# Hybrid block, software pipeline of 16 batches: the three filling steps rewritten with their own banks, places and orders, LayerNorms of those steps applied on ScalarE, and PSUM fetches of the draining steps moved to VectorE

## The reference

```python
x = x + attn_a(layernorm(x), w_qkv, w_out, b_out)   # 16 heads of 64: softmax(q*scale) over features,
                                                    # softmax(k) over tokens, context = q^T k per head,
                                                    # out = context applied to v, then @ w_out + b_out
x = x + ffn(layernorm(x), W_r, W_k, W_v, mu_r, mu_k)  # sigmoid(xr W_r) * (relu(xk W_k)^2 W_v)
                                                    # xr, xk: mu * x + (1 - mu) * (x shifted by a token)
x = x + attn_b(layernorm(x), W_Q, W_K, W_V, W_O)    # 16 heads of 8, rotary, softmax(q k^T / sqrt 8) v
x = x + ffn(layernorm(x), ... same weights)
```

## Time and profile before

| what | us |
|---|---|
| median of 3 runs (1088.19 to 1089.76) | 1088.46 |
| the profiled execution | 1087.98 |
| its span, first to last instruction of the program | 1086.2 |
| PE busy | 977.4 (90%) |
| ACT busy | 779.6 (72%) |
| DVE busy | 620.6 (57%) |
| POOL busy | 420.5 (39%) |

### The profile page before, as it was taken

The page is one execution under the profiler, slowest core; times in us unless marked ns, Lnnn a source line. Parts: engine busy times, 40 slices in busy tenths (PEclk is TensorE's granted clock), DMA queues, the critical chain, the costliest instruction groups (busy, mean ns, idle before and its releaser), DMA issues.

```text
span 1086.2 us, 21449 instructions
## 1 busy us (share of the span) xinstructions
PE 977.4 (90%) x8311; PEld 537.0 (49%) x8311; DVE 620.6 (57%) x1508; ACT 779.6 (72%) x905; POOL 420.5 (39%) x306
## 2 busy tenths in 40 slices
PE   3786798999999999999999999999999999999983
PEld 2565443545455454545455454545455454443322
DVE  4467644656675655656675655656675645564221
ACT  2343467787878687787878688787878687789861
POOL 3453534252625343352625344352625343223000
PEclk9899899999999999999999999999999999999985
DMA  5011121222223131222223131222222131322300
GB/s 152 20 31 49 50 80 38 70 68 72 75 59 98 54 97 37 72 68 69 78 60 97 55 97 36 73 65 72 75 60 88 51 90 37 96 66 84 83 24 15
DMA packets 61938, 72.25 MB, mean 67 GB/s; under 512 B 12289, under 2 KB 38786, under 8 KB 61826
## 3 DMA queue, kind: packets, MB, share of 16 engines
q1 hardware_dynamic: 61826, 70.75, 22.3%
HBM read 16.19 MB, written 20.97 MB: 34 GB/s over the span
## 4 chain that ended last, share of the span: by engine, by line
PE 66%; ACT 14%; DVE 12%; issue 4%; POOL 2%; SPq 1%; DMA 0%; ACTq 0%; DVEq 0%; POOLq 0%
PE PS L1279 17%; PE PS L1096 7%; PE PS L1235 6%; PE PS L1098 5%; PE PS L1097 5%; PE PS L1091 4%; ACT work L539 4%; PE PS L1152 4%; PE PS L1196 3%; PE PS L1203 3%; PE PS L1173 3%; ACT hn L567 2%; PE PS L1190 2%; ACT work L544 2%; ACT work L546 2%
## 5 line engine op out<-in xcount | busy, mean ns | idle before, releaser
L539 ACT ACTIVATE work<-PS 128x2048 f32<-128x2048 f32 x208 | 390.6, 1878 | 0.5 <-PE PS L1235 0.4
L533 ACT ACTIVATE work<-PS 128x512 f32<-128x512 f32 x256 | 152.6, 597 | 206.2 <-PE PS L1098 203.4
L1279 PE MATMUL PS<-work,v 128*32 128x512 f32 x2048 | 275.5, 610 | 2.8 <-DVE U L866 2.3
L375 POOL TENSOR_TENSOR rs<-ve,half_neg 128x4 f32<-128x4 f32 x64 | 65.3, 1020 | 368.1 <-DVE ve L724 368.1
L388 POOL TENSOR_TENSOR work<-work,q_rcp 128x1024 f32<-128x1024 f32 x64 | 121.8, 1903 | 173.0 <-DVE q_rcp L776 172.9
L1096 PE MATMUL PS<-wqk,h1h 128*128 128x512 f32 x256 | 123.0, 481 | 27.4 <-ACT gate L577 13.4
L1235 PE MATMUL PS<-q_st,k_st 32*128 32x512 f32 x832 | 105.6, 497 | 0.2
L1098 PE MATMUL PS<-wqk,h1l 128*128 128x512 f32 x256 | 102.8, 401 | 0.0
L1097 PE MATMUL PS<-wqk,h1h 128*128 128x512 f32 x256 | 102.4, 400 | 0.0
L773 DVE TENSOR_REDUCE q_sum<-work 128x16 f32<-128x1024 f32 x64 | 77.7, 1213 | 26.9 <-ACT work L533 26.7
L1152 PEld LDWEIGHTS PS<-work 128*64 128x64 f32 x2048 | 66.1, 140 | 47.3 <-ACT work L533 32.8
(11 more groups left out here) (144 smaller groups left out, 1667.7 us busy)
## 6 DMA issues: line engine op xcount, KB each, us to landing
qkv_scratch<-qkv_sb SPq DMA_DIRECT2D x16, 768.0 KB, 3.6
k_st<-k_hi SPq DMA_DIRECT2D x128, 64.0 KB, 2.1
k_st<-k_lo SPq DMA_DIRECT2D x128, 64.0 KB, 2.1
q_st<-q_hi SPq DMA_DIRECT2D x128, 64.0 KB, 2.1
q_st<-q_lo SPq DMA_DIRECT2D x128, 64.0 KB, 2.1
...
```

The source lines that it names most:

```text
L375: pool.tensor_tensor(rs[:, :], ve[:, :], half_neg[:, :], ALU.pow).then_inc(rstd[n].sem, 1)
L533: act.activation((EQ, EK)[r // 2][c % 2][:, (r % 2) * 512:(r % 2) * 512 + 512], PS[:, bank, :], ACT.Exp)\
L539: act.activation(probs[n % 2], PS[:, 0:4, :], ACT.Exp).then_inc(z["s_exp"].sem, 1)
L1279: mm = pe.matmul(PS[32 * h:32 * h + 32, 6, :], v_flat[p][:, kc, at:at + 32], probs[n % 2][:, h, :], start=(n % 8 == 0), stop=(n % 8 == 7), ...
```

## The change

1. **Start.** DVE makes `ones_col` and `ones8` first, and the copies into `wo_perm` last. ACT does the squares of a half of the weights right after its copy. The four memsets of the value tiles leave POOL's start and come as `clear_values` at the end of its step 0.
2. **Filling steps** (`filling_step` on every engine). The three LayerNorms applied there (n = 0, 1, 2) are applied by ACT (`ln_apply`) from a shift that DVE computes (`ln_shift`). Orders on all engines are new, `places(0..2)` are new, `ctx_wout` to `ffn_v` use banks 4 and 6 instead of 5 and 7, and the projections of stage l alternate between banks 7 and 4, two in a place. The small weights of step 0 are copied in two parts. `rsqrt_var(2, …)`, which step 2 ran last, runs first in step 3.
3. **Draining steps**: `p_copy`, `scale_mu` (as `scale_and_mix`) and LayerNorm 3 (as `ln_norm(3, …)`) go from ACT to DVE.
4. **All steps with stage l from step 3 on**: `norm_maxima` stands behind both `split_kq` instead of ahead of them.

The diff, cut; the three `filling_step` functions stand in the order GpSimd, VectorE (behind `first_step`), TensorE (of it only the end of the loop).

```diff
-                return Places(h1T=8, h3T=3, pb=4, hT1=10, k1=12, r1=13, kT=13, qT=14, v1=15)
+                return Places(c1=11, T=3, M=5, Y=6, h1T=9, h3T=5, pb=6, hT1=12, k1=15, r1=15, kT=15, qT=15, v1=15, mid=6)
...
+            dve.wait_ge(const_ok.sem, 4)
+            dve.tensor_copy(ones_col[:, :], one[:, :]).then_inc(ones_ok.sem, 1)
+            dve.tensor_copy(ones8[:, :], ones8f[:, :]).then_inc(b_ok.sem, 1)
             ln1_stats(0)
             ln1_norm(0)
...
+            def clear_values():
+                for t in range(2):
+                    pool.memset(v32[t][:, :, :, :], 0.0).then_inc(v0_ok.sem, 1)
...
+            def filling_step(i, p):
+                a, s, l = i, i - 1, i - 2
+                if at_batch(i, 0):
+                    rsqrt_var(0, 1)
+                if at_batch(i, 1):
+                    pool.wait_ge(b_ok.sem, 4)
+                if there(l):
+                    rsqrt_var(2, l)
+                if there(s):
+                    add_bias(s)
+                q_hats(a, 0)
+                if i >= 1:
+                    rsqrt_var(0, a + 1)
+                q_hats(a, 1)
+                if there(s):
+                    rsqrt_var(1, s)
+                if there(l):
+                    hold(pool, p_ev, l)
+                    rope_by_cos(att[0], l)
+                    rope_by_sin(att[0], l)
+                q_hats(a, 2)
+                split_h1(a + 1, 1 - p)
+                q_hats(a, 3)
+                if there(s):
+                    square(ffn[0], s)
+                if there(l):
+                    v_copy(att[0], l, p)
+                    squares(l)
+                if at_batch(i, 0):
+                    clear_values()
...
+            def ln_apply(n, j, src, dst):
+                hold(act, shift_ok[n], j - 1 if n == 0 else j)
                 for c in range(NC):
+                    act.activation(dst[:, c, :], src[:, c, :], ACT.Identity, bias=shifts[n][:, c:c + 1],
+                                   scale=stats[n][3][:, c:c + 1]).then_inc(ln[n].sem, 1)
...
+            def first_step():
+                ln1_stats(1)
+                ln_shift(0, 1)
+                sums_of(0, 0)
+                small_weights()
+                sums_of(0, 1)
+                split_weights()
+                sums_of(0, 2)
+                sums_of(0, 3)
+
+            def filling_step(i, p):
+                a, s, l = i, i - 1, i - 2
+                L, f1, z = there(l), ffn[0], att[0]
+                mid = places(i).mid
+                c_norm(s)
+                if L:
+                    ln_shift(2, l)
+                sums_of(a, 0)
+                ln1_stats(a + 1)
+                if L:
+                    split_h3(l)
+                ln_shift(0, a + 1)
+                sums_of(a, 1)
+                add_x1(s, mid)
+                ln_shift(1, s)
+                sums_of(a, 2)
+                if L:
+                    rope_sum(z, l)
+                mix(f1, s, mid)
+                if L:
+                    split_kq(z, l, 0)
+                sums_of(a, 3)
+                if L:
+                    split_kq(z, l, 1)
+                end_ffn1(s, mid)
+                if L:
+                    norm_maxima(l)
...
+            def scale_and_mix(f, j):
+                hold(dve, f["hT"], j)
+                for n in (1, 0):
+                    dve.tensor_scalar(f["mixed"][n][:, :], PS[:, 7, :], mu[:, n:n + 1], None, ALU.mult)\
+                       .then_inc(f["mu"].sem, 1)
+                mix(f, j)
+
+            def p_copy(j, c):
+                hold(dve, p_mm, j, c + 1)
+                dve.tensor_copy(qkv_sb[:, c, :], PS[:, 7, 0:W3]).then_inc(p_ev.sem, 1)
...
+                    if n == at.k1 and S:
+                        hold(pe, h1_sb, a + 1)
+                        ffn_k(f1, s)
+                    if n == 15:
+                        hold(pe, ph_exp, a, 12)
+                        context(a, 2)
+                    if n == at.kT and L:
+                        hold(pe, p_ev, l)
+                        kq_T(z, l, 0)
+                    if n == at.r1 and S:
+                        ffn_r(f1, s)
+                    if n == at.qT and L:
+                        hold(pe, z["split"], l, 2)
+                        kq_T(z, l, 1)
+                    if n == at.v1 and S:
+                        hold(pe, f1["mix"], s)
+                        ffn_v(f1, s, at.mid)
```

310 lines of the change are left out of this document (208 added, 102 removed).

## The result

The changed kernel takes 1061.66 us (median of 4 runs, 1061.35 to 1062.42), the kernel before, run beside it, 1088.33 (1086.96 to 1089.76). The ratio is 0.9756, with a 95% interval of 0.9739 to 0.9773. The forecast was 1069, its range 1056 to 1080: faster as forecast, and 7.3 us more of it. The span of the profiled execution is 1059.6 us.

The account below looks back on a forecast made before the run. PE was taken to set the full steps, with the gain in the short steps at both ends: -23.9 (start to step 2) + 2.5 (step 3) + 2.3 (draining) = -19.1 us, forecast 1069, range 1056 to 1080.

Parts of the forecast that it names:

- the rival in which the port is free in the draining steps: Norms slip in before POOL's rotation; steps 16 and 17 win 2.5 us together instead of losing 5.5: 1061, chance 0.13.
- Start: PE's first projection, with the ones cast before x arrives: at 14.9 us, bounds 14.4 and 17, 6.9 earlier.
- Step 0: First filling step: PE work 19.5 us, wait 2.4 and low clock 1.5, ending at 38.3 against 48.6.
- The anchor, x of batch 1: Step 0: its landing at 19.7 sets the first context, not before 26.2; PE waits 2.4 us.
- an earlier landing: Step 0: x of batch 1 landing before the forecast 19.7 was listed as a sign the prediction is wrong.
- Step 1: Filling step: 28.6 us against 29.1, with waits of 0.7, 0.5 and, at the end for POOL's square, 2.5.
- Step 2: Filling step: 29.1 us of PE work plus 8.4 of waits, 37.5 against 50.6.
- Steps 3 and 4: Only step 3 was charged: 2.5 us, for ctx_hd coming 1 us late and a low clock after the preceding stall.
- Twelve steps times zero: Full steps: moving norm_maxima costs nothing, since DVE waits 2.47 us for PE there; uncovered, up to 1.5 each.
- Draining: Steps 16 to the last: 3 and 2.5 us lost, 2.5 and 0.7 won, in sum 2.3 us slower.
- The scaling out of PSUM: Draining steps, moved to DVE: taken as 0.69 us without a row; at most 1.4 us in a step hang on it.
- the 5.5 us charged to steps 16 and 17: Draining steps: loss of 3 and 2.5 us from DVE's norms held by POOL's rotation through the shared port.

Follow-up runs that it names:

- the last kernel: Changed kernel with norm 3 and fetch back on ACT, norm_maxima ahead of the splits, square and k transposes earlier, x of batch 1 loaded early: 1049.98 us, ratio 0.9634.
- s_ones: Changed kernel with DVE's casts of the ones put back behind the weights' arrival and the wo_perm copies ahead of them: 1065.31 us, ratio 0.9791.
- s_xa: Changed kernel with x of batch 1 loaded earlier, between the loads of W_v and W_Q: 1061.85 us, ratio 0.9754.
- f_square: Changed kernel with POOL's square ahead of the fourth q_hats in the filling steps: 1060.34 us, ratio 0.9739.
- d_all: Changed kernel with the whole draining part undone (norm 3, fetch and scaling back on ACT): 1061.03 us, ratio 0.9749.
- d_scale_only: Changed kernel with norm 3 and the fetch of the projections back on ACT in the draining steps, only the scaling on DVE: 1054.35 us, ratio 0.9680.
- m_ahead: Changed kernel with norm_maxima put back ahead of both splits from step 3 on: 1059.83 us, ratio 0.9734.
- d_fetch: Changed kernel with only the fetch of the projections back on ACT in the draining steps: 1063.06 us, ratio 0.9769.
- d_norm: Changed kernel with only LayerNorm 3 of the draining steps applied by ACT again: 1058.13 us, ratio 0.9729.

## Why the prediction was right, and where its terms were off

Most of the mechanisms held; the total was too careful by 7.3 us. The measured 1061.7 lies inside the range but below the forecast's own band (1063 to 1075), and next to the 1061 of the rival in which the port is free in the draining steps. That is a coincidence: the port was not free, as the rows of step 17 show, and the time came from the front and from step 18. In the span (7.5) 5.1 of it came by the beginning of step 3, 0.7 in the steps from 5 on (674.2 us in all instead of 674.9), 1.8 in the draining steps, and 0.1 went the other way in steps 3 and 4.

- **Start.** Forecast 14.9, measured 14.09, below the lower bound of 14.4. The chain was right: the first norm matmul came at 9.61 (9.9 forecast), the reduction 1.91 later, the projection 2.57 after that. The 0.5 us allowed for the split of h1 were not needed. The profile does name `h1l` as what PE waited for, but it ended at 13.65, 0.4 us before the projection, and the distance of 2.57 from the reduction is the same before the change and in the last kernel, where `h1l` ended 1.4 us before. POOL's h1h did take 2.11 us, beside DVE's low parts of the weights; the same instruction took 1.04 in step 1. What the account lacks is why the cast of the ones had taken 4.76 us: it credits the order on DVE with the whole 6.9, and s_ones gives it 4.1 of the 7.7 measured.
- **Step 0.** Forecast 23.4, measured 21.3. The anchor, x of batch 1, is confirmed by s_ones and s_xa, at 19.1 instead of 19.7, and the wait was 2.1 for 2.4 forecast. By the letter an earlier landing was a sign of being wrong, but 0.6 us are less than its spread with the same code (18.5 to 20.1). No low clock followed it, so the 1.5 us allowed for one were not needed; f_square, with the same code, had one. My sentence that a start at 14.4 or at 17 ends in the same place was too strong: s_ones started 4.1 later and ended its step 0 2.2 later, since PE's work is longer than what is left once the wait is used up.
- **Step 1.** 28.6 forecast, 27.8 measured. The wait at the end was 1.8, not 2.5, behind POOL's fourth `q_hats` as described.
- **Step 2.** 37.5 forecast, 36.1 measured; waits of 3.8 for `k_act` (4.1 forecast), 1.0 for `ctx_hd` (1.3), 1.1 for the mixture (0.7), 0.6 for the split of k (1.2) and 0.3 for ACT's norm (1.1). All five are the ones forecast; most are a little shorter. The longest is the one at the place 15, and f_square shows its cause (the order on POOL). What the prediction did not see is that this wait was nearly free: the stacks for step 3 land no earlier. By my account, taking it away would have paid 3.8 us; it paid nothing in steps 2 and 3 until the splits of k and q came earlier.
- **Steps 3 and 4.** Charged 2.5 in step 3, measured 1.2 in step 3 and 1.4 in step 4: the right sum from a wrong working, which is luck. The wait for `ctx_hd`, put at 1 us in step 3, was 0.2. The 1.2 is low clock at the head of step 3, as forecast: in d_all and d_scale_only, with the same code there, the low stretch lasts 3.4 instead of 6.8 us and the step takes 62.5 and 62.4. The 1.4 is `norm_maxima`, which I costed at "Twelve steps times zero". It held for eleven of them and failed in the first: I took the cover of 2.47 us from a full step and didn't read the one in step 3, 0.47.
- **Full steps.** Zero forecast, zero measured: 61.0 in both, and in m_ahead.
- **Draining.** +2.3 forecast, +0.5 measured. Step 17's mechanism is confirmed row by row (6.20 us for "some 6", PE waiting 3.6 us for `U`); it cost 3.5, not 2.5, since a low clock came with it. Step 16 was sized right (2.5 for 3) with half a cause: there PE waited for the norm of x1, which the fetch moved onto the rotation, and norm 3 only takes over as the cause when the fetches are gone (d_fetch). Step 18 won 4.6, not 2.5: I counted waits and left the clock, which is 1.00 in every kernel with less on ACT in this step (0.91 before and in d_all), out of the sum. That term is the largest mis-sized one of the draining steps.
- **The scaling out of PSUM**, taken at 0.69, took 0.75 and hid behind idle time; it took two instructions a step (1.2 us) from ACT in step 18.

The prediction drew on the Trainium skill ("SBUF — State Buffer", Who interferes with whom), by which leaving the norm on ACT would be worth the 5.5 us charged to steps 16 and 17. The trace agrees on the mechanism: 1.10 us against 6.20 for the same four instructions, and ACT's own norm in d_norm takes 1.64 beside the same rotation. In size it was 4.5 us in step 17 and, as long as the fetches stayed on DVE, nothing in step 16.

What stays open: the low clock behind a wait of 2 to 4 us comes in some executions and not in others (step 0 of f_square had 3.4 us of it behind a wait of 2.8, the changed kernel none behind 2.1; both have the same code there), and no run here separates the length of the wait from what PE did before it.
